# A maximum over eight heads taken in two halves, in the first attention of a four-layer kernel

## The chip, the cores and the metric

The kernel is one program on one core of a Trainium2 chip. Its five engines run their own queues and meet through semaphores: TensorE (PE in the rows, its weight loads PEld) multiplies, VectorE (DVE), ScalarE (ACT) and GpSimd (POOL) work on tiles, and SyncE (SP) issues most transfers. The metric is the device time of one execution in microseconds.

## What is computed

Four layers run one after the other: an attention with relative positions, a deep feed-forward and local-attention stack, a causal attention and a mixture of experts. Only the first is touched:

```python
B, S, D = x.shape                      # 16, 256, 128; H = 16 heads of hd = 8
q, k, v = (proj(Wq), proj(Wk), proj(Wv))
content = jnp.einsum('bhld,bhmd->bhlm', q, k)
rel_k = jnp.einsum('bhld,lmd->bhlm', q, a_k)
rel_q = jnp.einsum('bhmd,lmd->bhlm', k, a_q)
logits = (content + rel_k + rel_q + pos_pos) * scale
attn = jax.nn.softmax(logits, axis=-1)
out = jnp.einsum('bhlm,bhmd->bhld', attn, v) + jnp.einsum('bhlm,lmd->bhld', attn, a_v)
```

The softmax subtracts the maximum of each row of 256 logits before it takes the exponential.

## The kernel before

The first attention works through 16 sequences of 256 tokens. A sequence has four groups g: two blocks of 128 rows (`lt = g // 2`) by two sets of eight heads (`g % 2`). The logits of a group are a tile of 128 rows by 8 heads by 256 columns in SBUF, `logits`. Every engine's order is written out by hand in its function `sequence`, once for the first, the looped and the last sequence; semaphores with counted values tie the engines together.

For one group the work goes like this. TensorE's `scores` writes the products into four banks (L648, L652, L658), `between` them other work for the next sequence (L570 turns x, L577 projects, L598 spreads the keys). VectorE's `add_keyed` adds them into `logits` in two additions (L908), then `maxima` takes the maximum of all eight heads in one reduction (L913) and multiplies it by the negative scale (L916, called the negative here). ScalarE's `exps` takes eight exponentials, one for each head, in two calls of four (L797), each with a column of `nbias`. TensorE's `turn` transposes four heads at a time (L674), ScalarE's `turns` copies them out (L803), and `outputs` multiplies them with the values (L699). VectorE masks these (L948), sums them (L957, L960) and scales them (L963).

Two banks, the `ring`, serve everything else that TensorE writes: x, the projections, the queries with their keys (L609 and L612, copied out by ScalarE at L814), the outputs `y`, and the spread keys `kb` (L598, masked out by VectorE at L940). Each entry waits until the one two places before it is out. So L598 in group 2 waits for VectorE's L948, as does L570, which turns x for the next sequence.

GpSimd works beside them: `far_keys` copies edge values into the logits of the next sequence (L502, L504, after short operations L497 and L500), L519 builds the diagonal keys once the scores of a group are through, and L537 and L540 place the values.

VectorE's order in a looped sequence: maximum of group 1, `outputs(0)`, group 2 with its maximum, `sums(0)`, `outputs(1)`, `blocks`, `sums(1)`, `blocks`, group 3 with its maximum, `outputs(2)`, `sums(2)`, `blocks` and the additions of the next sequence's group 0, its maximum, `outputs(3)`, `sums(3)`.

Of the kernel before, what the change touches and what calls it, by code (L numbers as in the profile page):

```python
# [21 lines left out]
ALU = mybir.AluOpType  # L22
ACT = mybir.ActivationFunctionType
AX = mybir.AxisListType
# [6 lines left out]
SCALE_A = 1.0 / HD ** 0.5  # L31
# [100 lines left out]
def build_program(nc, T, out):  # L132
    ctx = ExitStack()
    with ctx:
        def sb(stack, name, shape, dt=F32):
            return stack.enter_context(nc.sbuf_tensor(name, shape, dt))

        def sem(name):
            return ctx.enter_context(nc.semaphore(name))
# [101 lines left out]
        with ExitStack() as st:  # L241
# [26 lines left out]
            logits = sb(st, "a_logits", [P, LT, H, S])  # L268
# [8 lines left out]
            nmax = sb(st, "a_nmax", [P, 8])  # L277
            nbias = sb(st, "a_nbias", [P, 8])
# [23 lines left out]
            with nc.Block() as block:  # L302
# [130 lines left out]
                def _(pe):  # L433
# [8 lines left out]
                    for i in range(6):  # L442
# [22 lines left out]
            score_full, logit_ok, bias_ok, exp_done = (sem("a_score_full"), sem("a_logit_ok"), sem("a_bias_ok"),  # L465
                                                       sem("a_exp_done"))
# [21 lines left out]
            with nc.Block() as block:  # L488
# [64 lines left out]
                def _(pe):  # L553
                    def sequence(part, b):
# [18 lines left out]
                        def project_groups(names, rep):  # L573
                            for name in names:
                                r, full = room(name)
                                for j in range(2):
                                    last = nc.tensor.matmul(r[:, j * S:(j + 1) * S],  # L577
                                                            rep[:, 2 * name[1] + j, :, :].rearrange("p a c -> p (a c)"),
                                                            xT[:, :], start=(j == 0), stop=(j == 1), skip_group_check=True)
                                last.then_inc(full, 1)  # L580

                        def project_v():
                            r, full = room("v")
                            for t in range(LT):
                                last = nc.tensor.matmul(r[:, t * D:(t + 1) * D], xT[:, t * P:(t + 1) * P], wv[:, :],
                                                        start=(t == 0), stop=(t == 1), skip_group_check=True)
                            last.then_inc(full, 1)

                        def spread_block(name):

                            if name is None:
                                return

                            out_of(ks[name[1] // 4])
                            r, full = room(name)
                            for j in range(2):
                                h = 2 * name[1] + j
                                last = nc.tensor.matmul(r[:, j * S:(j + 1) * S], sum_k[:, h % 4, :], k_parts[:, h // 4, :],  # L598
                                                        start=(j == 0), stop=(j == 1), skip_group_check=True)
                            last.then_inc(full, 1)  # L600
# [15 lines left out]
                        def scores(g, seq):  # L616

                            lt, hg = g // 2, g % 2
                            if g == 0:
                                pe.wait_ge(queries_ok, seq + 1)  # L620
                            if lt == 0:
                                pe.wait_ge(diag_ok, seq * 4 + 2 * hg + 2)

                            def between(i):

                                if g == 1 and i == 0:
                                    turn(0, 1)
                                if part != "loop":
                                    return
                                if g == 1 and i in (1, 2):  # L630
                                    project_groups(ks[i - 1:i], wk_rep)
                                if g == 1 and i == 3:
                                    project_v()
                                if g == 3 and i < 2:
                                    spread_block(kb[2 + i])
                                if g == 0:
                                    spread_block(kb[4 + i])

                            o = [score[:, kq, :].rearrange("p (h m) -> p h m", h=8) for kq in range(4)]

                            def contents(kq):

                                if g > 0 or not isinstance(seq, int) or seq > 0:
                                    at = 3 * (seq * 4 + g - 1) + kq // 2 + 1
                                    pe.wait_ge(logit_ok, at)
                                for i in range(2):
                                    hq = 2 * hg + i
                                    nc.tensor.matmul(o[kq][:, 4 * i:4 * i + 4, :], q_parts[:, hq, lt * P:(lt + 1) * P],  # L648
                                                     k_diag[:, 4 * hq:4 * hq + 4, kq * 64:(kq + 1) * 64],
                                                     start=(i == 0), stop=False, skip_group_check=True)  # L650
                                    if kq == 3 - 3 * lt:
                                        last = nc.tensor.matmul(o[kq][:, 4 * i:4 * i + 4, :], e_parts[:, lt, :],  # L652
                                                                k_diag[:, 4 * hq:4 * hq + 4, kq * 64:(kq + 1) * 64],
                                                                start=False, stop=(i == 1), skip_group_check=True)
                                for n in range(4) if kq != 3 - 3 * lt else ():
                                    blk = kq * 4 + n
                                    v = lt * P - blk * LB + S - LB
                                    last = nc.tensor.matmul(o[kq][:, :, n * LB:(n + 1) * LB], eq_tab[:, v:v + P],  # L658
                                                            k_blk[:, 8 * hg:8 * hg + 8, blk * LB:(blk + 1) * LB],
                                                            start=False, stop=(n == 3), skip_group_check=True)  # L660
                                last.then_inc(score_full, 1)

                            for kq in range(4):
                                contents(kq)
                                between(kq)

                        def turn(g, half):
                            pe.wait_ge(exp_done, b * 8 + 2 * g + half + 1)
                            for mt in range(LT):

                                if half == 1:
                                    pe.wait_ge(turn_out, b * 16 + 4 * g + mt + 1)
                                for h in range(4):
                                    last = nc.tensor.transpose(turned[mt][:, h * P:(h + 1) * P],  # L674
                                                               logits[:, g // 2, 8 * (g % 2) + 4 * half + h,
                                                                      mt * P:(mt + 1) * P], ident[:, :])
                                last.then_inc(turn_full, 1)
# [85 lines left out]
                def _(act):  # L763
                    def sequence(part, b, norm=False):
# [26 lines left out]
                            nc.scalar.copy(v_next, r[:, 0:LT * D].rearrange("p (t c) -> p t c", t=LT)).then_inc(free, 1)  # L791

                        def exps(g, half, seq):
                            act.wait_ge(bias_ok, seq * 4 + g + 1)
                            for h in range(4 * half, 4 * half + 4):
                                row = logits[:, g // 2, 8 * (g % 2) + h, :]
                                last = nc.scalar.activation(row, row, ACT.Exp, bias=nbias[:, h:h + 1], scale=SCALE_A)  # L797
                            last.then_inc(exp_done, 1)
# [91 lines left out]
                def _(dve):  # L890
# [4 lines left out]
                    def sequence(part, b, norm=False):  # L895
# [13 lines left out]
                                "p k (h m) -> p h k m", h=8), at, ALU.add).then_inc(logit_ok, 1)  # L909

                        def maxima(g, seq):
                            dve.wait_ge(logit_ok, 3 * (seq * 4 + g) + 2)
                            nc.vector.tensor_reduce(nmax[:, :], logits[:, g // 2, 8 * (g % 2):8 * (g % 2) + 8, :],  # L913
                                                    AX.X, ALU.max).then_inc(logit_ok, 1)
                            dve.wait_ge(logit_ok, 3 * (seq * 4 + g) + 3)
                            nc.vector.tensor_scalar(nbias[:, :], nmax[:, :], -SCALE_A, None, ALU.mult).then_inc(bias_ok, 1)  # L916

                        def add_and_maxima(g, seq):
                            add_keyed(g, seq, 0)
# [1133 lines left out]
        with ExitStack() as st:  # L2053
# [6 lines left out]
            nmax = sb(st, "c_nmax", [P, 2, 4])  # L2060
# [778 lines left out]
```

## Time and profile before

| | us |
|---|---|
| median of 3 runs | 5165.76 |
| lowest, highest | 5158.77, 5169.23 |
| profiled execution | 5161.43 |
| its span | 5159.6 |
| TensorE, VectorE busy over the span | 4641.8 (90%), 3703.7 (72%) |
| ScalarE, GpSimd busy over the span | 3408.9 (66%), 3562.0 (69%) |
| first attention, its 16 sequences | from about 69 to 1110 |

A row of the timeline gives when an instruction (or a run of like ones, x4) started, how long it took, its engine and line, what it writes and reads, and in square brackets how long the engine was idle before it and which instruction ended that. The busy shares are means over four layers with different limits; the first attention is a fifth of the span.

### The profile page before, as it was taken

To read this page: it belongs to the slowest core of one execution; us is meant where nothing else is said; L and a number is where in the kernel's file an instruction comes from. 1 tells how busy PE (TensorE), PEld (TensorE's weight loads), DVE (VectorE), ACT (ScalarE), POOL (GpSimd) and SP (SyncE) were. 2 spreads that over 40 slices of the span, in tenths; PEclk is the share of its full clock that TensorE was granted. 3 is DMA by queue.
4 is the path that set the end of the run, shared out by engine and by line. 5 is a ranking of instruction groups with operands and counts; after the bars stand their busy time and mean duration, and the time that the engine had idled before them with its cause. 6 is when DMAs were issued, how large, how long until landed. Compare 5 with 4: busy or idle time off the path is not lost. (4 is left out here: it accounts for less than half of the span.)

```text
span 5159.6 us, 202579 instructions
## 1 busy us (share of the span) xinstructions
PE 4641.8 (90%) x82160; PEld 3806.8 (74%) x82160; DVE 3703.7 (72%) x7406; ACT 3408.9 (66%) x6468; POOL 3562.0 (69%) x2507
## 2 busy tenths in 40 slices
PE   6888878879999999999999999999999997788879
PEld 4767666667887788878887888788887886555557
DVE  4666666668887788878887888778877885555543
ACT  3555555547777777777777777777777775566664
POOL 3333333349999999999999999999999995222212
PEclk8999999989999999999999999999999998898889
DMA  3333333323222322232223222232223222000000
GB/s 103 90 90 90 91 91 91 91 74 82 69 69 70 86 69 69 68 88 71 68 70 86 71 69 70 73 83 69 69 71 73 69 70 49 1 0 0 0 1 17
DMA packets 500474, 339.02 MB, mean 66 GB/s; under 512 B 222560, under 2 KB 489085, under 8 KB 499214
## 3 DMA queue, kind: packets, MB, share of 16 engines
q1 hardware_dynamic: 493566, 320.55, 24.5%
q10 hardware_dynamic: 6544, 13.18, 0.8%
q8 instruction: 282, 4.62, 0.4%
q14 instruction: 82, 0.66, 0.0%
HBM read 60.06 MB, written 54.58 MB: 22 GB/s over the span
## 5 line engine op out<-in xcount | busy, mean ns | idle before, releaser
L1401 POOL TENSOR_TENSOR b_rnorm<-b_ss,neghalf 128x16 f32<-128x16 f32 x384 | 1119.1, 2914 | 24.2 <-DVE b_ss L1937 20.2
L1397 POOL TENSOR_TENSOR b_rot<-b_t 128x1024 f32<-128x1024 f32 x384 | 910.0, 2370 | 75.5 <-DVE b_t L1926 74.6
L1924 DVE TENSOR_TENSOR b_t<-psum,b_cosg 128x1024 f32<-128x1024 f32 x384 | 469.6, 1223 | 422.9 <-ACT b_sq L1779 416.9
L1408 POOL TENSOR_TENSOR b_qk<-b_rot,b_rnorm 128x1024 f32<-128x1024 f32 x384 | 731.6, 1905 | 42.8 <-POOL b_rnorm L1401 2.7
L1525 PE MATMUL psum<-b_w_hi,b_xT_parts 128*128 128x512 f32 x1152 | 529.4, 460 | 25.8 <-issue 17.6
L1779 ACT ACTIVATE b_sq<-psum 128x1024 f32<-128x1024 f32 x384 | 392.9, 1023 | 222.4 <-PE psum L1530 222.1
L1931 DVE TENSOR_REDUCE b_ss_floor<-b_sq 128x16 f32<-128x1024 f32 x384 | 464.4, 1209 | 0.0
L1530 PE MATMUL psum<-b_w_hi,b_xT_parts 128*128 128x512 f32 x1152 | 461.0, 400 | 0.0
L1526 PE MATMUL psum<-b_w_lo,b_xT_parts 128*128 128x512 f32 x1152 | 457.8, 397 | 1.2 <-issue 1.2
L1612 PE MATMUL psum<-shared,b_oT 128*128 128x128 f32 x3072 | 425.3, 281 | 0.8 <-ACT b_oT L1797 0.8
L1514 PE MATMUL psum<-ident,b_qk 128*128 128x128 f32 x3072 | 408.0, 276 | 10.1 <-DVE b_o L1963 9.9
L1514 PEld LDWEIGHTS psum<-ident,b_qk 128*128 128x128 f32 x3072 | 362.9, 142 | 71.5 <-DVE b_o L1963 19.3
L797 ACT ACTIVATE a_logits<-a_logits,a_nbias 128x256 f32<-128x256 f32 x512 | 216.8, 500 | 287.4 <-DVE a_nbias L916 286.9
L1612 PEld LDWEIGHTS psum<-shared,b_oT 128*128 128x128 f32 x3072 | 379.9, 191 | 27.0 <-issue 1.1
L1802 ACT ACTIVATE b_pr<-b_pr 128x512 f32<-128x512 f32 x384 | 241.9, 630 | 212.7 <-DVE b_pr L1947 195.0
L1963 DVE TENSOR_TENSOR b_o<-psum,b_rs 128x256 f32<-128x256 f32 x768 | 326.2, 425 | 26.4
L1622 PE MATMUL psum<-b_v_win,b_prT 64*32 64x65 f32 x24576 | 336.0, 225 | 5.9 <-issue 5.9
L1593 PE MATMUL psum<-b_kT,b_qTs 64*32 64x64 f32 x24576 | 333.2, 224 | 0.0
L1639 PE MATMUL psum<-b_xnT,b_w 128*128 128x256 f32 (+1 forms) x1152 | 308.2, 390 | 17.2 <-DVE b_hid L1987 2.9
L1593 PEld LDWEIGHTS psum<-b_kT,b_qTs 64*32 64x32 f32 x24576 | 270.5, 105 | 61.3 <-issue 50.1
L1622 PEld LDWEIGHTS psum<-b_v_win,b_prT 64*32 64x32 f32 x24576 | 271.4, 105 | 53.8 <-issue 7.4
L1797 ACT COPY b_oT<-psum 128x512 f32<-128x512 f32 x384 | 232.5, 606 | 111.3 <-PE psum L1560 111.3
(271 smaller groups left out, 11673.1 us busy)
## 6 DMA issues: line engine op xcount, KB each, us to landing
b_v_win<-b_v SPq DMA_DIRECT2D x2304, 65.0 KB
keyed<-shared SPq DMA_DIRECT2D x64, 768.0 KB, 4.1
b_v_win<-b_v SPq DMA_DIRECT2D x1152, 32.5 KB
a_logits<-keyed SPq DMA_DIRECT2D x128, 160.0 KB, 3.2
oa<-XR SPq DMA_DIRECT2D x1024, 2.0 KB
xcur<-X SPq DMA_DIRECT2D x111, 128.0 KB, 4.3
shared<-in_L_ffn_Wqkv_dram ACTq DMA_DIRECT2D x6, 1536.0 KB
a_logits<-keyed SPq DMA_DIRECT2D x64, 128.0 KB, 3.3
```

What stands on the lines that cost most here:

```text
L1397: nc.gpsimd.tensor_tensor(rot[:, i, :, :], t1[:, i, :, :], t2[:, i, :, :], ALU.add).then_inc(rot_done, 1)
L1401: nc.gpsimd.tensor_tensor(rnorm[:, i, :], ss[:, i, :], neghalf[:, :], ALU.pow).then_inc(rn_done, 1)
L1408: nc.gpsimd.tensor_tensor(qk[:, i, :, :], rot[:, i, :, :], rnorm[:, i, :, None].broadcast_to((P, 16, BD)), ALU.mult).then_inc(qk_done, 1)
L1514: last = nc.tensor.transpose(r[:, p * P:(p + 1) * P], qk[:, s % 2, a * 8 + 2 * p:a * 8 + 2 * p + 2, :].rearrange("p h d -> p (h d)"), iden ...
L1525: nc.tensor.matmul(r, xT_hi[:, ts], w_hi[:, piece(hg, i)], start=True, stop=False)
L1526: nc.tensor.matmul(r, xT_hi[:, ts], w_lo[:, piece(hg, i)], start=False, stop=False)
L1530: return nc.tensor.matmul(r, xT_lo[:, ts], w_hi[:, piece(hg, i)], start=False, stop=True)
L1593: last = nc.tensor.matmul(bank[3 + j][qs, p * 2 * WIN:(p + 1) * 2 * WIN], qTs[at, p, qs], kT[at, p, keys], start=False, stop=(p == 3), ski ...
L1612: last = nc.tensor.matmul(bank_c[:, 0:D], oT[:, p, :], wo[:, 4 * (s % SEQ // 2) + p, :], start=(p == 0), stop=(p == 3))
L1622: last = nc.tensor.matmul(r[qs, p * (BD + 1):(p + 1) * (BD + 1)], prT[at, p, qs], v_win[at, s % NV, c, p, :], start=(p == 0), stop=(p == 3 ...
L1924: nc.vector.tensor_tensor(t14, x4, tab(cosg, slice(0, BD), BD), ALU.mult)
L1931: nc.vector.tensor_reduce(ss_floor[:, t, :, 0], sq[:, :].rearrange("p (h d) -> p h d", d=BD), AX.X, ALU.add).then_inc(ss_done, 1)
```

## The change

The maximum is taken over four heads, then its negative, then the same for the other four. `bias_ok` counts two per group instead of one, so that the exponentials of a half wait for their own negative, and `logit_ok` counts four instead of three, which renumbers TensorE's wait in `contents`. The bytes read and written are the same; VectorE has two more instructions per group, 128 in all.

```diff
@@ TensorE, contents
-                                    at = 3 * (seq * 4 + g - 1) + kq // 2 + 1
+                                    at = 4 * (seq * 4 + g - 1) + kq // 2 + 1
@@ ScalarE, exps
-                            act.wait_ge(bias_ok, seq * 4 + g + 1)
+                            act.wait_ge(bias_ok, 2 * (seq * 4 + g) + half + 1)
@@ VectorE, maxima
-                            dve.wait_ge(logit_ok, 3 * (seq * 4 + g) + 2)
-                            nc.vector.tensor_reduce(nmax[:, :], logits[:, g // 2, 8 * (g % 2):8 * (g % 2) + 8, :],
-                                                    AX.X, ALU.max).then_inc(logit_ok, 1)
-                            dve.wait_ge(logit_ok, 3 * (seq * 4 + g) + 3)
-                            nc.vector.tensor_scalar(nbias[:, :], nmax[:, :], -SCALE_A, None, ALU.mult).then_inc(bias_ok, 1)
+                            for half in range(2):
+                                hs = slice(4 * half, 4 * half + 4)
+                                dve.wait_ge(logit_ok, 4 * (seq * 4 + g) + 2 + half)
+                                nc.vector.tensor_reduce(nmax[:, hs], logits[:, g // 2, 8 * (g % 2) + 4 * half:
+                                                                            8 * (g % 2) + 4 * half + 4, :],
+                                                        AX.X, ALU.max).then_inc(logit_ok, 1)
+                                dve.wait_ge(logit_ok, 4 * (seq * 4 + g) + 3 + half)
+                                nc.vector.tensor_scalar(nbias[:, hs], nmax[:, hs], -SCALE_A, None,
+                                                        ALU.mult).then_inc(bias_ok, 1)
```

VectorE's queue in the looped sequences, from the last addition of group 0 to the masking of the outputs of group 3, before (in the changed kernel the lines behind stand four higher, so L948 is L952 there):

```order
184 L908 TENSOR_TENSOR a_logits<-psum,a_logits 128x8x128
185 L912 ISA
186 L913 TENSOR_REDUCE a_nmax<-a_logits 128x8
187 L915 REGISTER_ALU
188 L916 TENSOR_SCALAR a_nbias<-a_nmax 128x8
189 L898 REGISTER_ALU
190 L948 TENSOR_TENSOR a_ymask<-psum,a_own 128x432 x2
```

The same place in the changed kernel:

```order
211 L908 TENSOR_TENSOR a_logits<-psum,a_logits 128x8x128
212 L914 ISA
213 L915 TENSOR_REDUCE a_nmax<-a_logits 128x4
214 L918 REGISTER_ALU
215 L919 TENSOR_SCALAR a_nbias<-a_nmax 128x4
216 L915 TENSOR_REDUCE a_nmax<-a_logits 128x4
217 L918 REGISTER_ALU
218 L919 TENSOR_SCALAR a_nbias<-a_nmax 128x4
219 L898 REGISTER_ALU
220 L952 TENSOR_TENSOR a_ymask<-psum,a_own 128x432 x2
```

A second maximum and a second negative stand between the first negative and the masking; nothing else changes its place on any engine.

## Rows read from the trace of the kernel before

**Rows 1.** The head of the page: the span of the whole execution.

```profile
span 5159.6 us, 202579 instructions
```

**Rows 2.** Windows, 69 to 1110: busy us of each engine, PEclk, DMA, GB/s.

```profile
69.00:1110.00 1041.00, 836.12 (x12340) 725.08 (x12344) 692.41 (x907) 532.40 (x1171) 329.46 (x506) 0.93 0.32 89
```

**Rows 3.** By line: duration min/median/max in ns, or busy us and mean ns.

```profile
L913 DVE TENSOR_REDUCE a_nmax<-a_logits x64: 2286/2286/2286, 77.7 to 1099.9; 128x8 f32<-128x2048 f32 x64
...
L916 DVE TENSOR_SCALAR a_nbias<-a_nmax x64: 171/188/617, 80.0 to 1102.2; 128x8 f32<-128x8 f32 x64
...
L1931 DVE TENSOR_REDUCE b_ss_floor<-b_sq 128x16 f32<-128x1024 f32 x384 | 464.4, 1209 | 0.0
```

**Rows 4.** Timeline, group 2 of one sequence, all engines: start us, us, engine, line.

```profile
305.64 3.75 POOL L519 TENSOR_TENSOR a_k_diag<-a_k_parts,a_head_rows 128x1024 fp32r<-128x1024 f32 x2 [2.13 <-PE psum L658]
306.85 2.29 DVE L913 TENSOR_REDUCE a_nmax<-a_logits 128x8 f32<-128x2048 f32 x1
309.17 0.24 DVE L916 TENSOR_SCALAR a_nbias<-a_nmax 128x8 f32<-128x8 f32 x1
309.36 1.69 DVE L957 TENSOR_REDUCE a_ysum<-a_ymask 128x72 f32<-128x864 f32 x1
309.45 3.31 ACT L797 ACTIVATE a_logits<-a_logits,a_nbias 128x256 f32<-128x256 f32 x8 [7.12 <-DVE a_nbias L916]
...
311.20 1.09 PE L674 MATMUL psum<-ident,a_logits 128*128 128x128 f32 x8 [3.03 <-ACT a_logits L797]
...
312.81 0.30 PEld L598 LDWEIGHTS psum<-a_k_parts,a_sum_k 128*128 128x128 f32 x2 [0.28 <-DVE a_ymask L948]
...
313.27 0.90 PEld L674 LDWEIGHTS psum<-ident,a_logits 128*128 128x128 f32 x8 [0.17 <-ACT a_probsT L803]
```

**Rows 5.** Timeline, group 0, a sequence where the negative met GpSimd's copies early.

```profile
536.91 2.34 POOL L537 COPY a_values<-shared 128x544 f32<-128x544 f32 x4
536.97 0.60 DVE L916 TENSOR_SCALAR a_nbias<-a_nmax 128x8 f32<-128x8 f32 x1
537.48 1.11 DVE L948 TENSOR_TENSOR a_ymask<-psum,a_own 128x432 f32<-128x432 f32 x2
```

**Rows 6.** Timeline, group 3 of the sequence of rows 4.

```profile
318.83 3.75 POOL L519 TENSOR_TENSOR a_k_diag<-a_k_parts,a_head_rows 128x1024 fp32r<-128x1024 f32 x2 [9.44 <-PE psum L658]
...
320.05 2.29 DVE L913 TENSOR_REDUCE a_nmax<-a_logits 128x8 f32<-128x2048 f32 x1
...
322.81 1.25 POOL L502 COPY a_logits<-shared 128x1280 f32<-128x1280 f32 x1
...
323.20 0.61 DVE L948 TENSOR_TENSOR a_ymask<-psum,a_own 128x432 f32<-128x432 f32 x1 [0.60 <-PE psum L699]
...
323.87 0.45 PE L609 MATMUL psum<-a_ek_diag,a_q_next 128*128 128x384 f32 x1 [0.18 <-DVE a_ymask L948]
```

**Rows 7.** Timeline, group 0 of the next sequence; last, TensorE's loop turning over.

```profile
271.82 2.29 DVE L913 TENSOR_REDUCE a_nmax<-a_logits 128x8 f32<-128x2048 f32 x1
...
273.04 2.34 POOL L537 COPY a_values<-shared 128x544 f32<-128x544 f32 x4
...
274.14 0.17 DVE L916 TENSOR_SCALAR a_nbias<-a_nmax 128x8 f32<-128x8 f32 x1
274.24 1.12 DVE L948 TENSOR_TENSOR a_ymask<-psum,a_own 128x432 f32<-128x432 f32 x2
...
274.90 0.44 PE L570 MATMUL psum<-ident,xcur 128*128 128x128 f32 x2 [2.10 <-DVE a_ymask L948]
...
276.10 1.97 PE L674 MATMUL psum<-ident,a_logits 128*128 128x128 f32 x8 [0.77 <-ACT a_logits L797]
...
406.86 0.68 PE L570 MATMUL psum<-ident,xcur 128*128 128x128 f32 x2 [4.34 <-issue]
```

**Rows 8.** Timeline, TensorE: transposes in a looped sequence (group 2) and the last one.

```profile
443.61 1.97 PE L674 MATMUL psum<-ident,a_logits 128*128 128x128 f32 x8 [3.03 <-ACT a_logits L797]
...
1090.11 1.09 PE L674 MATMUL psum<-ident,a_logits 128*128 128x128 f32 x8 [2.97 <-ACT a_logits L797]
```

## The prediction

> **What bounds the kernel now.** The profiled execution spans 5159.6 us [rows 1] and took 5161.4; the median of the runs shown is 5165.8. The change touches the first attention alone, 69 to 1110 us of the trace, so I read that stage. By the windows TensorE is busy 836 of 1041 us there, VectorE 692, ScalarE 532, at a mean granted clock of 0.93 [rows 2]: no engine is full, and the stage goes at the pace of a chain that passes from one engine to the next. The next view is therefore the timeline of one sequence (about 64.8 us; there are 16, four groups each), read for what each TensorE wait is put down to. Three places matter:
>
> - Group 2: the maximum ends, the negative follows, ScalarE starts its eight exponentials at 309.45, TensorE transposes from 311.20. Behind that stands the row to notice: the loads of L598 wait for VectorE's L948, up to 312.81, and only 0.17 us of waiting for ScalarE is left at 313.27 [rows 4]. VectorE's own queue (maximum, L957, L948) is already the last to arrive at L598, and at the next transposes ScalarE and VectorE come in almost together.
> - Group 3: L609 waits for L948 at 323.87, and ScalarE's copies of what L609 makes stand ahead of the second half's exponentials in its queue [rows 6].
> - Group 0 of the next sequence: VectorE's L948 frees the bank in which TensorE turns x (L570, a wait of 2.10 us), then the transposes wait 0.77 us for ScalarE [rows 7].
>
> **The change, part by part.** *Pieces.* One maximum of 2286 ns becomes two of 1024 elements. L1931, another reduction, of 1024 elements, takes 1209 ns [rows 3]; 2286 is 2048 elements and a rest, so two halves are 2.42 to 2.44 us: 0.15 dearer. The negative's shortest is 171 ns [rows 3], and one follower starts about 0.10 us behind it at 274.24 [rows 7] (the negative stands at 274.14, 2.32 us after the maximum began). So undisturbed, the first negative ends 1.25 + 0.17 = 1.42 us after the maximum starts, where now it is 2.49: **1.07 us earlier**. The work behind it starts at 2.71 instead of 2.42: **0.29 us later**. The second half's negative (2.8) is there before the first four exponentials are through (1.42 + 1.62, four of eight in 3.3 us). The two waits for numbers of the semaphore are renumbered and hold nobody back.
>
> *Who stands beside it.* In groups 2 and 3 GpSimd runs L519, two operations in 3.75 us, started by the same end of the scores that starts VectorE's last addition: 305.64 for a maximum at 306.85. The negative at 309.17 takes 0.24, not 0.17, and ends at 309.41, when L519 ends (309.39) [rows 4]. At 536.97 it takes 0.60 us and ends with the first of four copies of L537 (one is 0.6 us), begun 0.06 us ahead of it; L948 behind it starts only then [rows 5]. I read this as: the negative waits until GpSimd's operation is over, and VectorE's queue waits with it. Before, all but 0.07 us of that was covered by the length of the maximum itself. The split moves the first negative 1.07 us forward, into the middle of the operation. The longest hold that a row shows is 0.60 - 0.17 = 0.43; a negative that starts at 308.10 and ends with L519 at 309.41 would be held for 1.31 - 0.17 = 1.14. Bounds for one such hold: 0 and 1.14; I take all of it, since every row ends with the GpSimd operation however it began.
>
> The Trainium skill has this as a rule ("SBUF — State Buffer", section "SBUF: two separate sides"): VectorE and GpSimd share a pair of ports as an exclusive lock, and the loser blocks for the whole instruction; it names VectorE operations in a two-port mode and those with two inputs in SBUF. "VectorE: DVE Perf Modes", section "Mode 2×_2P — use both read ports for one tensor", puts an fp32 tensor_scalar from SBUF to SBUF in that mode. The trace agrees by the 0.24 and 0.60 above. By the rule the sum is the one below; without it, that of the first rival.
>
> *Group 2.* The first half ends at 308.07, its negative is held to 309.41, where the whole one ends today: the exponentials gain nothing. The second half runs 309.36 to 310.6, its negative after L519 is free, and L957 starts at 310.70 instead of 309.36: VectorE is 1.34 us late. L948, and with it the loads of L598, come at 314.15 instead of 312.81; their own 0.29 brings the transposes of the second half to 314.44 instead of 313.27: **+1.2 us**. That is the case in 11 of 15 sequences. In the other four TensorE does the eight transposes at half speed, 1.97 us [rows 8] instead of 1.09, and comes some 0.5 us later to L598, so VectorE's lateness costs about **0.75**. Sum 13.2 + 3.0 = 16.2 us.
>
> *Group 3.* L519 and the maximum move by the same 1.2 us and lie alike: the first negative is again held to L519's end (323.8), the second half ends at 325.0, and its negative meets L502, a copy of 1.25 us that begins then 0.2 us behind L519 (322.81 today, 324.01 then) and is held to 325.28. L948 starts near 325.25 instead of 323.20: 2.05 late, 0.85 more than TensorE. L609 has to wait for it. Of this some 0.2 is taken back, as the first four exponentials no longer delay ScalarE's copies. I take **+0.6**, between 0 and 1.0: 9.0 us in 15 sequences.
>
> *Group 0.* The half ends 1.22 us after the start, exactly where L537 begins (273.04 for 271.82). As at 536.97 the first negative is held to the first copy's end: ready at 1.87 instead of 2.49. The second lands between copies and ends at about 3.2, L948 starts 0.7 us later (0.3 to 1.1), L570 at 275.6 instead of 274.90. TensorE no longer waits the 0.77 us for ScalarE, so the transposes start at 275.9 instead of 276.10: **-0.2** (-0.6 to +0.35), 12 times: -2.4. At two further turns TensorE's own loop holds L570 for 4.34 us [rows 7], and nothing changes.
>
> *Group 1* of the 15: the first exponentials start earlier, but TensorE's L609 and ScalarE's copies set the pace behind; 0.
>
> *First and last sequence.* Here nothing of VectorE is behind the transposes: TensorE waits 2.97 us for the exponentials at 1090.11 [rows 8], more in the first sequence, and GpSimd is idle: 1.07 gained four times, 0.6 once (group 0 with L537 beside it): -4.9.
>
> **Sum** 16.2 + 9.0 - 2.4 - 4.9 = **+17.9 us**: 5179.3 against 5161.4, and 5183.7 on the median. ScalarE's and GpSimd's instructions stay; SP's stores and reads stay in order and move with the sums. The later stages keep their instructions.
>
> **Rivals.**
>
> (1) *Faster: the negative isn't held.* If a 128x4 negative slips in beside L519, VectorE is only 0.29 us late. Group 2 then still doesn't gain (L598 waits on VectorE: about +0.1), group 3 gains 0.2, group 0 gains 0.6 x 12 = 7, the ends 5.3: 13 us, and about 2 more where the shorter wait spares TensorE its half speed: 5150. For it: at 274.14 a negative ran in 0.17 while L537's copies ran. Against: it stood at the seam of two copies (1.10 us after the first began, and four take 2.34), and each negative beside L519 in groups 2 and 3 ends with it. It decides when the hold is under some 0.3 us. Chance 0.13.
>
> (2) *No difference: the clock gives it back.* TensorE's granted clock falls to half after its waits, in two places in nearly every sequence: the eight transposes at 276.10 take 1.97 us, those at 1090.11 take 1.09. The mean of 0.93 over 1041 us [rows 2] is 0.07 x 2 x 1041 = 146 us at the lower level, 1.2 GHz, and 73 us of work not done in them. Waits that move by 2 us per sequence can lose some of these stretches or gain some. A seventh of them lost is 10 us and brings +18 to +8, inside what can be told apart; as much gained brings +28. A smaller hold in group 3 (0 instead of 0.6) also ends at +9. Chance 0.23, time near 5172.
>
> (3) *The hold is dearer*: both group 0 (+0.35) and group 3 (+1.0) at their upper ends and 1.34 in each group 2: 20 + 15 + 4 - 5 = +34, 5200. It is part of the forecast's side.
>
> **How the numbers follow.** The forecast with (3) has 0.64. A measurement of this kernel tells about 0.2% (10 us) from no change. Slower by over 0.2%: 0.64, within: 0.23, faster: 0.13. The predicted time is 5184. The range reaches from 5157 (below rival 2, most of rival 1 left out) to 5202 (rival 3).
>
> **What would show it.** In the timeline of the changed kernel, first negatives of groups 2 and 3 of 1.1 to 1.3 us that end with L519, and second negatives of group 3 held by L502; if the longest is under 0.3 us, rival 1 holds. The exponentials of group 2 start no earlier against the maximum's start (2.6 us after it), and TensorE's wait in front of L598 grows from 0.28 us to over 1 us. In group 0 L570's wait grows from 2.10 to near 2.8, and the 0.77 for ScalarE goes. The last sequence is 4 us shorter. A sequence of the loop takes 66.3 us instead of 64.8. The prediction is wrong in its main step if sequences are as long as now or shorter, and wrong by the clock if holds are as said, yet the stage's mean clock is far from 0.93.

## The result, and the profile after

The changed kernel takes 5200.43 us (median of 4 executions, 5197.28 to 5209.0), the kernel before 5162.92 (4, with one more run than above): a ratio of 1.0074, with an interval of 1.0057 to 1.0092. It is slower by 37.5 us. The forecast was slower, at 5184, in a range up to 5202. The profiled execution took 5200.61, against 5161.43. One number further down needs a word: of the twelve executions of the kernel in which ScalarE makes the negatives, one took 7589 us at a mean granted clock of 0.77 (the others had 0.95 to 0.96), and it is left out of that kernel's ratio.

First the page of the changed kernel: its span [rows 1], and the busy time of the engines with the count of their instructions.

```profile
span 5198.8 us, 202811 instructions
...
PE 4655.9 (90%) x82160; PEld 3825.4 (74%) x82160; DVE 3749.8 (72%) x7534; ACT 3409.6 (66%) x6468; POOL 3562.2 (69%) x2507
```

VectorE has 128 instructions more and is busy 46 us longer; TensorE has the same number of matmuls and is busy 14 us longer, as part of them run at a lower clock. The last run of products (L699) of the first attention starts at 1146.59 us of the trace, where it started at 1112.83: 33.8 of the 39.2 us of longer span arise in this stage. The same view as [rows 2], over the changed kernel's stage (PEclk is the third figure from the end, 0.90):

```profile
69.00:1147.00 1078.00, 859.37 (x12433) 752.05 (x12432) 737.47 (x1036) 532.22 (x1169) 327.36 (x502) 0.90 0.31 85
```

The mean granted clock fell from 0.93 to 0.90. By line, as [rows 3], duration min/median/max in ns:

```profile
L915 DVE TENSOR_REDUCE a_nmax<-a_logits x128: 1205/1218/1222, 73.1 to 1137.2; 128x4 f32<-128x1024 f32 x128
...
L919 DVE TENSOR_SCALAR a_nbias<-a_nmax x128: 170/333/1375, 74.4 to 1138.5; 128x4 f32<-128x4 f32 x128
```

Two halves are 2.44 us, as worked out. The negative of four elements, whose shortest is 170 ns, takes up to 1375. The timeline of one ordinary sequence shows where it is long. First group 2, as [rows 4] (start us, us, engine, line; idle time and its end in brackets).

```profile
580.46 3.75 POOL L519 TENSOR_TENSOR a_k_diag<-a_k_parts,a_head_rows 128x1024 fp32r<-128x1024 f32 x2 [2.14 <-PE psum L658]
581.67 1.22 DVE L915 TENSOR_REDUCE a_nmax<-a_logits 128x4 f32<-128x1024 f32 x1
...
582.93 1.31 DVE L919 TENSOR_SCALAR a_nbias<-a_nmax 128x4 f32<-128x4 f32 x1
584.15 1.21 DVE L915 TENSOR_REDUCE a_nmax<-a_logits 128x4 f32<-128x1024 f32 x1
584.27 3.30 ACT L797 ACTIVATE a_logits<-a_logits,a_nbias 128x256 f32<-128x256 f32 x8 [7.12 <-DVE a_nbias L919]
585.39 0.17 DVE L919 TENSOR_SCALAR a_nbias<-a_nmax 128x4 f32<-128x4 f32 x1
585.57 1.71 DVE L961 TENSOR_REDUCE a_ysum<-a_ymask 128x72 f32<-128x864 f32 x1
...
586.03 1.97 PE L674 MATMUL psum<-ident,a_logits 128*128 128x128 f32 x8 [3.03 <-ACT a_logits L797]
...
588.48 1.08 PEld L598 LDWEIGHTS psum<-a_k_parts,a_sum_k 128*128 128x128 f32 x4 [0.88 <-DVE a_ymask L952]
588.48 1.37 PE L598 MATMUL psum<-a_k_parts,a_sum_k 128*128 128x256 f32 x4 [0.48 <-DVE a_ymask L952]
```

L519 ends at 584.21, and so does the negative (584.24). The exponentials start 2.60 us after the maximum did, as before, and L961 3.90 us after it, where L957 started 2.51 after: VectorE is 1.39 us late. The transposes start 4.36 us after the maximum, as before (4.35), but take 1.97 us instead of 1.09. Group 3, as [rows 6]:

```profile
596.29 3.75 POOL L519 TENSOR_TENSOR a_k_diag<-a_k_parts,a_head_rows 128x1024 fp32r<-128x1024 f32 x2 [12.08 <-PE psum L658]
...
598.76 1.30 DVE L919 TENSOR_SCALAR a_nbias<-a_nmax 128x4 f32<-128x4 f32 x1
...
600.28 1.26 POOL L502 COPY a_logits<-shared 128x1280 f32<-128x1280 f32 x1
...
601.22 0.33 DVE L919 TENSOR_SCALAR a_nbias<-a_nmax 128x4 f32<-128x4 f32 x1
...
602.12 0.45 PE L609 MATMUL psum<-a_ek_diag,a_q_next 128*128 128x384 f32 x1 [0.96 <-DVE a_ymask L952]
```

The first negative ends with L519 (600.04), the second with L502 (601.54), and L609 waits 0.96 for L952 where it waited 0.18. Group 0 of the next sequence, as [rows 7]:

```profile
615.90 2.34 POOL L537 COPY a_values<-shared 128x544 f32<-128x544 f32 x4
615.92 0.63 DVE L919 TENSOR_SCALAR a_nbias<-a_nmax 128x4 f32<-128x4 f32 x1
616.47 1.21 DVE L915 TENSOR_REDUCE a_nmax<-a_logits 128x4 f32<-128x1024 f32 x1
...
617.71 0.55 DVE L919 TENSOR_SCALAR a_nbias<-a_nmax 128x4 f32<-128x4 f32 x1
618.17 1.11 DVE L952 TENSOR_TENSOR a_ymask<-psum,a_own 128x432 f32<-128x432 f32 x2
...
618.82 0.44 PE L570 MATMUL psum<-ident,xcur 128*128 128x128 f32 x2 [3.16 <-DVE a_ymask L952]
```

Both negatives are held, each to the end of a copy of L537 (616.5, and 618.24 with the last), and L570 waits 3.16 instead of 2.10. The wait of 0.77 in front of the transposes is gone.

**A sequence against a sequence**, both from one L570 to the next (274.90 to 339.76 before, 550.49 to 618.82 after): 64.86 us became 68.33.

The starts that bound the stretches are 274.90, 300.55, 311.20, 320.26, 334.97 and 339.76 before, and 550.49, 575.38, 586.03, 597.73, 612.97 and 618.82 after.

| stretch | before | after | differs | forecast |
|---|---|---|---|---|
| L570 to the transposes of group 1's second half | 25.65 | 24.89 | -0.76 | -0.2 less what is late at L570 |
| to group 2's transposes | 10.65 | 10.65 | 0 | 0 |
| to the L609 of group 3 that waits 0.81 for ScalarE | 9.06 | 11.70 | +2.64 | +1.2 |
| to the first L699 of group 3 | 14.71 | 15.24 | +0.53 | +0.6 |
| to the next L570 | 4.79 | 5.85 | +1.06 | +0.7 |

One stretch is far from its forecast, the one that holds group 2's transposes. The granted clock there, in windows of 1 us of TensorE (us, busy, PEclk), of the changed kernel and then of the kernel before, each around its transposes (586.03 and 311.20):

```profile
584.00:585.00 1.00, 0.00 (x0) 1.00 0.00 0
585.00:586.00 1.00, 0.00 (x0) 0.66 0.00 0
586.00:587.00 1.00, 0.97 (x5) 0.50 0.00 0
...
591.00:592.00 1.00, 1.00 (x7) 0.50 0.07 4
592.00:593.00 1.00, 1.00 (x10) 0.92 0.07 4
```

```profile
310.00:311.00 1.00, 0.00 (x0) 1.00 0.00 0
311.00:312.00 1.00, 0.80 (x7) 1.00 0.00 0
312.00:313.00 1.00, 0.90 (x6) 1.00 0.03 2
```

Behind the same wait of 3.03 us (3.1 in the first two sequences) the changed kernel's TensorE runs some 6.8 us at the lower level, 1.2 GHz, in 14 of 15 sequences, and 3.4 in the other; before, it stayed at 2.4 GHz in 11 of 15, and the other four had 3.4 us. In two of the changed kernel's sequences, at 242.45 and 309.97, the clock falls 1.5 and 2.3 us after the transposes started, and these take 1.09 us; there L598 waits 1.37 us for VectorE, a second wait that the kernel before doesn't have in any sequence. From 60 us to the end of the stage, summed from windows of 0.5 us, TensorE spent 214.7 us at the lower level in 46 stretches, against 158.0 in 39.

### The profile page after: what moved, and what is told of

The parts are those of the page before. It is cut to its first block and busy times, and to the rows that moved or that the text cites. A ratio compares the mean times of both kernels' runs of the same rounds, so it can differ in the third digit from the quotient of the medians.

```text
span 5198.8 us, 202811 instructions
## 1 busy us (share of the span) xinstructions
PE 4655.9 (90%) x82160; PEld 3825.4 (74%) x82160; DVE 3749.8 (72%) x7534; ACT 3409.6 (66%) x6468; POOL 3562.2 (69%) x2507
```

## The experiments

Each is compared with executions of the kernel before that were timed beside it: their median was 5164.65 for the three kernels with one group halved and the one with ScalarE's negatives, 5164.04 for the next four, and 5165.14 for the four with added products. Theories: **A**, the hold of the negative by GpSimd's running operation makes VectorE late, and TensorE waits for that; **B**, the two halves or their waits cost by themselves, wherever they stand. The clock became a third question after the first traces; the expectations call it theory C: about half of the loss is TensorE at the lower clock behind group 2's wait.

### One group alone

The maxima of one group halved, of the others whole (the numbers on the semaphores follow), in 15 of the 16 sequences. The edit against the kernel before, with `(2,)`, `(3,)` or `(0,)`, shortened:

```diff
+            HALVED, HALVED_FIRST, HALVED_LAST = (2,), False, False
...
-                            nc.vector.tensor_reduce(nmax[:, :], logits[:, g // 2, 8 * (g % 2):8 * (g % 2) + 8, :],
+                            parts = (slice(0, 4), slice(4, 8)) if halved(g, seq) else (slice(0, 8),)
+                            for n, hs in enumerate(parts):
...
```

> Only group 2 of the looped sequences is halved (15 times). Theory A (the first negative is held by GpSimd's L519, so VectorE comes 1.34 us late to L598, and TensorE, waiting longer, loses more at half speed): about 2.6 us a sequence as in the changed kernel's trace, +39 us; the hold without the clock would be 1.2 a sequence, +18. Theory B (two more VectorE instructions per group cost what they cost, 0.29 us, GpSimd has no part): under +5 us.

> Only group 3 is halved (15 times). Theory A: both negatives are held, L609 waits for VectorE, +0.5 to +0.6 us a sequence, +9 us. Theory B: the first exponentials come 0.8 us earlier and the copies behind with them, -3 us to 0.

> Only group 0 of the looped sequences is halved (15 times). Theory A: held by L537's copies, L570 one us late, some of it given back as TensorE no longer waits for the exponentials: +0.3 us a sequence, 0 to +10 us. Theory B: -0.6 us a sequence, -8 us.

Measured: group 2 alone 5199.19 us, ratio 1.0067 [1.0045, 1.0088], **+34.5**; group 3 alone 5186.71, 1.0051 [1.0035, 1.0066], **+22**; group 0 alone 5166.22, 1.0006 [0.9998, 1.0015], **+1.6**. Group 2 is near what A expected with the clock in it (+39). Group 3 costs more than twice its forecast, and the three come to 58 where all together cost 37.5: the medians don't add. In the stage of group 3's kernel the windows give 200 us at the lower clock in 45 stretches, where the kernel before has 158 in 39, and not at group 3 alone: from 614.8 the clock is low for 6.8 us behind group 0's wait, which the edit doesn't touch, where the kernel before has 3.4. Halves that meet a copy of 0.6 us (group 0) cost next to nothing. B had expected under +5, at most 0, and -8 us: it is wrong in groups 2 and 3, and group 0's interval leaves its -8 out as well.

### VectorE late, without halves

Maxima whole, and behind the negative of group 2 a reduction that nobody reads:

```diff
+                            if g in (2,):
+                                nc.vector.tensor_reduce(idle[:, :], own[:, None, :].broadcast_to((P, 10, YW)),
+                                                        AX.X, ALU.max)
```

> The kernel before with whole maxima, and behind the negative of each group 2 a VectorE reduction of 1080 elements of a constant into a tile that nobody reads (about 1.28 us): VectorE is as late there as in the change, with no halves and no held negative. Theory A (only VectorE's lateness counts): the same as the kernel that halves group 2 alone, +35 to +40 us for 16 groups. If the held negative or the halves do more than make VectorE late: under +20 us.

Measured: 5193.03 us, 1.0058 [1.0044, 1.0072], **+29**. VectorE and TensorE in group 2:

```profile
584.66 1.26 DVE L919 TENSOR_REDUCE a_idle<-a_own 128x10 f32<-128x1080 f32 x1
585.85 1.70 DVE L961 TENSOR_REDUCE a_ysum<-a_ymask 128x72 f32<-128x864 f32 x1
```

```profile
586.54 1.68 PE L675 MATMUL psum<-ident,a_logits 128*128 128x128 f32 x8 [3.03 <-ACT a_logits L798]
588.74 1.37 PE L599 MATMUL psum<-a_k_parts,a_sum_k 128*128 128x256 f32 x4 [0.52 <-DVE a_ymask L952]
```

An ordinary 1.19 us of lateness (584.66 to 585.85) costs 29 us where group 2's halves alone cost 34.5. That is under the +35 to +40 expected, and so is the lateness under the 1.39 us of the changed kernel; it is well over the +20 below which the halves or the hold would have had a cost of their own. So most of the loss is lateness, whatever makes it, and it is paid for dearly: 1.8 us per sequence for 1.19. Here too TensorE runs at the lower clock behind group 2's wait in all 15 looped sequences: in nine the transposes are slowed (1.64 to 1.97 us), in six they take 1.09 and the clock falls 1.0 to 2.4 us after they started, in the wait of L599 for VectorE or just behind it.

### The holder shortened

GpSimd's L519 over 32 of its 256 columns in the loop, with whole maxima and with halved ones. These two leave out the rest of the diagonal keys.

```diff
-                            nc.gpsimd.tensor_tensor(k_diag[:, hq * 4:hq * 4 + 4, :],
...
+                            w = S if part == "first" else 32
+                            nc.gpsimd.tensor_tensor(k_diag[:, hq * 4:hq * 4 + 4, 0:w],
...
```

> The kernel before with GpSimd's L519 over 32 of 256 columns in the looped sequences (the keys of the other columns are left as the first sequence wrote them, which leaves work out): it is over long before any negative. L519 is on nobody's path: -3 to +1 us against the kernel before.

> The changed kernel with the same shortened L519 (work left out as in the kernel with whole maxima). Theory A: groups 2 and 3 have no held first negative, the loss of some 45 us there goes, what is left is group 0 (+5) and the gain of the ends (-5): within 5 us of the kernel before, at best -10. Theory B: still +25 us or more.

Measured: whole 5199.19 us, 1.0066 [1.0052, 1.0079], **+35**; halved 5152.94, 0.998 [0.9971, 0.9989], **-11**. The second is as A had it: the first negatives of groups 2 and 3 are free, and the change loses nothing, though group 3's second negatives are still held by L502 (0.8 us in most sequences). GpSimd also has less work there, so this run alone doesn't prove A. The first is a plain miss. Its trace shows a hold that wasn't foreseen. GpSimd and VectorE in group 3 (L917 is the negative, L914 the maximum there):

```profile
599.19 1.25 POOL L502 COPY a_logits<-shared 128x1280 f32<-128x1280 f32 x1
```

```profile
597.09 2.29 DVE L914 TENSOR_REDUCE a_nmax<-a_logits 128x8 f32<-128x2048 f32 x1
599.41 1.06 DVE L917 TENSOR_SCALAR a_nbias<-a_nmax 128x8 f32<-128x8 f32 x1
```

L502 stands behind L519 in GpSimd's queue. With L519 short it starts before the maximum is through instead of behind the negative, and holds the negative for 1.06 us, to its own end (600.44 against 600.47). Here is the kernel before, without any halving, with a negative of 1.0 to 1.2 us in group 3 of all 15 looped sequences, and its ordinary sequences last 68.2 us instead of 64.8. In the one from 550.95 on, 2.4 of these 3.4 us lie in group 3 (17.1 us from the L609 that waits for ScalarE to L699, before 14.7), with a stretch at the lower clock in them that the kernel before doesn't have there. The hold was moved by the experiment, not taken away. That all 35 us come from it is argued, not shown.

### Only where GpSimd is idle

Halved: the first group of the first sequence, and groups 1 to 3 of the last.

```diff
+            HALVED, HALVED_FIRST, HALVED_LAST = (), True, True
```

> Only the first group of the first sequence and groups 1 to 3 of the last are halved, where GpSimd is idle and TensorE waits 3 us or more for the exponentials. Both theories: four times -1.07 us, -4 us, at the edge of what can be measured; read from the trace: 1.07 us earlier from the maximum's start to the exponentials.

Measured: 5162.31 us, 0.9993 [0.9984, 1.0002], **-1.7**, inside what can't be told from nothing; the forecast of -4 isn't refuted. Its trace has what was to be read from it: the exponentials start 1.46 us after the maximum in these four groups, where they started 2.53 after it before, 1.07 earlier. In the changed kernel the last sequence, from the transposes of group 0 on, runs 46.9 us instead of 51.6 (1099.65 to 1146.59 and 1061.26 to 1112.83): its halves gain there, as forecast, but TensorE also spends 6.6 us less at the lower clock in it, so not all of the 4.6 us need be theirs.

### ScalarE makes the negatives

All maxima halved, and the negative taken from VectorE's queue:

```diff
+                                act.wait_ge(logit_ok, before_group(g, seq, 3) + 3 + n)
+                                nc.scalar.mul(nbias[:, hs], nmax[:, hs], -SCALE_A).then_inc(bias_ok, 1)
...
-                            nc.vector.tensor_scalar(nbias[:, :], nmax[:, :], -SCALE_A, None, ALU.mult).then_inc(bias_ok, 1)
```

> All groups are halved as in the change, but ScalarE makes the negatives (a multiplication ahead of its four exponentials). Nothing of VectorE can be held by GpSimd there any more, and VectorE's queue is 0.1 us longer than before instead of 1.3. Theory A: the loss is gone and the earlier exponentials show, -5 to -15 us against the kernel before. Theory B, or a cause in the halves or in the earlier exponentials: slower than before, +15 us or more.

Measured: 5155.75 us, 0.9979 [0.9969, 0.999], **-9**, against +37.5 for the same halves with VectorE's negatives. In group 2, across ScalarE and TensorE:

```profile
569.38 0.20 ACT L820 ACTIVATE a_nbias<-a_nmax 128x4 f32<-128x4 f32 x1 [5.78 <-DVE a_nmax L942]
569.62 1.71 ACT L824 ACTIVATE a_logits<-a_logits,a_nbias 128x256 f32<-128x256 f32 x4
```

```profile
571.38 1.09 PE L696 MATMUL psum<-ident,a_logits 128*128 128x128 f32 x8 [1.93 <-ACT a_logits L824]
573.42 1.37 PE L617 MATMUL psum<-a_k_parts,a_sum_k 128*128 128x256 f32 x4 [0.94 <-DVE a_ymask L976]
```

Beside the same running L519 ScalarE's negative takes 0.20 us, and the transposes wait 1.93 instead of 3.03. So the split does what it says as soon as its negatives are not VectorE's: 45 us against the change. (The profiled execution took 5164.39 us, 9 over the median.)

### TensorE kept at work in its waits

To separate the clock from the hold, products that nobody reads were put into TensorE's waits: 16 in front of group 2's transposes in the changed kernel and in the kernel before; in the kernel before also 12 in front of L570, where TensorE waits 2.10 us, and 10 in front of the L609 behind group 1's scores, where it waits 1.87; and 12, 10 and 10 in the kernel in which ScalarE makes the negatives. They write to a bank of the transposes, so the 10 have a wait for ScalarE's copies of group 0 ahead of them.

```diff
+                        def idle_products(count):
+
+                            for _ in range(count):
+                                nc.tensor.matmul(turned[0][:, 0:2 * KJ].rearrange("p (h j) -> p h j", h=2), unit[:, :],
+                                                 pp_parts[:, None, :].broadcast_to((P, 2, KJ)),
+                                                 start=True, stop=True, skip_group_check=True)
...
+                        idle_products(16)
```

> The changed kernel with 16 products that nobody reads (2.8 us at full speed) in TensorE's wait of 3.03 us ahead of group 2's transposes. What they fill is idle time, so the hold of VectorE stays as it is. Theory C (half of the loss is TensorE at half speed behind that wait, 6.8 us of it in each sequence): the stretches at group 2 go, and the kernel is 15 to 20 us faster than the changed one, about +16 us on the kernel before. If the whole loss is VectorE's lateness: no change, +37 us.

> The kernel before with the same 16 products at the same place. Only 4 of its sequences have the half-speed stretch there, 0.6 us each: -2 us under theory C, 0 otherwise; more than +5 would say that the products themselves cost something and weaken the other run.

> The kernel before with products that nobody reads in all three waits of TensorE: 12 ahead of turning x (2.1 us), 10 ahead of L609 (1.9 us), 16 ahead of group 2's transposes. Theory C: the 3.4 us at half speed behind each of the first two waits go in each sequence, 0.8 us saved in the transposes and about as much in the products of L577, up to 1 us at L609: -20 to -35 us. If half speed there is off the path: 0, and up to +5 where a product overruns a wait.

> Halves with ScalarE's negatives and products that nobody reads in the three waits (12, 10 and 10, as the wait at group 2 is 1.9 us here). Theory C: the gains add, -9 and -20 to -35: 5120 to 5135 us. If the waits or the half speed are not what bounds this one: near 5155.

| kernel | median us | ratio [interval] | against before |
|---|---|---|---|
| change, 16 products | 5165.60 | 1.0009 [0.9997, 1.0021] | +0.5 |
| before, 16 products | 5153.84 | 0.9983 [0.9970, 0.9995] | -11 |
| before, products in three places | 5148.53 | 0.9975 [0.9963, 0.9987] | -17 |
| ScalarE's negatives, products in three places | 5108.70 | 0.9895 [0.9880, 0.9910] | **-56** |

The changed kernel with 16 products, group 2, TensorE:

```profile
575.76 3.07 PE L725 MATMUL psum<-a_pp_parts,a_unit 128*128 128x384 f32 x16
578.87 1.09 PE L674 MATMUL psum<-ident,a_logits 128*128 128x128 f32 x8
581.33 0.30 PEld L598 LDWEIGHTS psum<-a_k_parts,a_sum_k 128*128 128x128 f32 x2 [1.60 <-DVE a_ymask L960]
581.33 1.08 PE L598 MATMUL psum<-a_k_parts,a_sum_k 128*128 128x256 f32 x4 [1.37 <-DVE a_ymask L960]
...
589.18 0.44 PE L609 MATMUL psum<-a_ek_diag,a_q_next 128*128 128x384 f32 x1 [0.82 <-ACT shared L822]
```

```profile
578.00:579.00 1.00, 0.96 (x6) 1.00 0.00 0
579.00:580.00 1.00, 0.96 (x8) 1.00 0.00 0
580.00:581.00 1.00, 0.00 (x0) 1.00 0.00 0
```

For VectorE nothing differs: the negative is held as before (1.30 us), the transposes start 4.36 us after the maximum, and the wait for VectorE at L598, 1.37 us, is now in the open. But the transposes take 1.09 us in all 15 looped sequences, and in 13 of them the clock stays at 2.4 GHz up to group 3. The change had lost 37.5 us; with the wait filled it is level with before. The products help the kernel before too (-11); its time at the lower clock falls from 158 to 128 us.

This splits group 2's term. From its transposes to the L609 that waits for ScalarE (578.87 to 589.18 here) there are, over 14 looped sequences of each kernel:

| kernel | us | seen in |
|---|---|---|
| before | 9.06 | 10 of 14; 9.6 to 9.9 in the four with slow transposes |
| before, 16 products | 9.05 to 9.13 | all |
| change | 11.5 to 12.8, mean 11.8 | all |
| change, 16 products | 10.1 to 10.3 | 12 of 14; 11.9 in the two where the clock falls later |

With the clock held up, VectorE's lateness costs 1.0 to 1.3 us a sequence; the rest of the loss there, about 1.4 us, is TensorE at the lower clock. Over the whole time, the two kernels with the wait filled lie 11.8 us apart by the medians, 18.4 by the spans of their profiled executions (5168.3 and 5149.9): the cost of the holds without the lower clock behind group 2's wait. By this difference the other 19 to 26 of the 37.5 us are that clock.

My expectation for the changed kernel (+16) was too high, that for the kernel before too small with products in one place (-2 expected), and too hopeful with products in three (-20 to -35). For the last the trace shows a cause. The products move the turns of the engines a little, and now group 1's negative meets a copy of GpSimd's (of three rows, GpSimd's, VectorE's and TensorE's):

```profile
551.77 1.25 POOL L504 COPY a_logits<-shared 128x1280 f32<-128x1280 f32 x1
551.87 1.18 DVE L929 TENSOR_SCALAR a_nbias<-a_nmax 128x8 f32<-128x8 f32 x1
553.61 0.44 PE L609 MATMUL psum<-a_ek_diag,a_q_next 128*128 128x384 f32 x1 [1.16 <-DVE a_ymask L961]
```

Group 1's negative takes 1.17 to 1.26 us in 15 of 16 sequences, where it took 0.17 before, and this L609 waits 1.16 us instead of 0.19. So -17 is a gain by the clock less a new hold. The last kernel has its negatives on ScalarE and so no such hold; it is the fastest of the study, and beats its forecast. Its windows over 14 sequences:

```profile
78.00:952.00 874.00, 778.77 (x11400) 678.80 (x11399) 600.29 (x809) 494.13 (x1159) 295.90 (x453) 1.00 0.34 93
```

TensorE is at 2.4 GHz nearly throughout, and sequences last 60.2 to 64.0 us, with a first period of 66.4. That is more than the two parts bring alone (-9 and -17), which the new hold in the one and the lower clock in the other explain at least in part: from 60 us on its stage has 37 us at the lower level, that of the kernel with ScalarE's negatives has 199 (in its profiled execution), that of the kernel before with products in three places 73.

## Why the prediction came out as it did

The direction and its cause were right, the size short by half: +17.9 forecast, +37.5 measured, inside the range by 2 us. That it is inside is luck: the upper end was rival 3's sum of dearer holds, and the loss came to that size by the clock. What the sum did price, holds with the clock unchanged, measured 12 to 18 us between the two kernels with group 2's wait filled.

- **The hold** is shown as the prediction put it. First negatives of groups 2 and 3 take 1.30 to 1.38 us and end with L519, second ones of group 3 are held by L502, and beside an idle GpSimd the same instruction takes 0.17. I took all of the 1.14 between 0 and 1.14: right. The loss fell away on ScalarE (-9 instead of +37.5) and with a short L519 (-11).
- **Pieces**: two halves take the 2.44 us worked out, and the exponentials of group 2 start no earlier.
- **Group 2** is the step that failed. The term was +1.2 in 11 sequences and +0.75 in four, which took the four that show half speed as given and the other eleven as staying at full speed. It measured +2.64 in the sequence shown. VectorE's 1.39 us of lateness is there, and with the clock held up it costs the +1.0 to +1.3 that was forecast; the transposes at 1.97 instead of 1.09 and everything behind them up to 592.2 at 1.2 GHz are what was missing. The wait of L598's loads grew from 0.28 to 0.88 us only (the products' to 0.48), not to over 1, because the slow transposes covered the rest; with the clock held up it is 1.60 (1.37). That sign of the prediction, taken alone, would have spoken against the right theory.
- **Group 3**: +0.53 against +0.6. In the sum of one sequence the term holds; as an experiment of its own it costs 22 us instead of 9, with 42 us more at the lower clock, part of it behind waits of other groups.
- **Group 0**: the path to L570 is 1.06 late (0.7 forecast, bounds 0.3 to 1.1), since the second negative is held as well; -0.76 comes back behind it. The net is +0.30 where -0.2 stood, inside its bounds; alone it measured +1.6 us.
- **Ends**: the last sequence is 4.6 us shorter from its group 0 on, some of it perhaps by the clock; the 1.07 us is in the trace, and timed alone the ends give -1.7, not to be told from zero.
- **Rival 1** (not held) is refuted by the rows. **Rival 2** named the right quantity and put the wrong sign first: the lower clock took 56.7 us more of the stage instead of giving some back. A seventh of 146 more, its losing side, had been priced at +28; it was over a third. **Rival 3** named +34 and came nearest to the size, but by another way: only group 0's hold is near its upper end, and what it put on the other holds is the clock's.

The mistake has a plain form: the sum priced a wait and its lateness at the mean clock, and then let the clock vary as a rival of its own. It should have stood in the term of group 2, since the trace already held its two cases: transposes of 1.09 and of 1.97 us after the same 3.03 us of waiting [rows 8], 11 and 4 times. The four could become fifteen, and did, once two of them are counted in which the clock falls only behind the transposes.

What stays open is why a TensorE that waits the same 3.03 us drops its clock in one kernel and keeps it in the other. The rows show that it does, that work in the wait prevents it, and that the kernels with a late VectorE have a second wait, at L598, right behind it: where the transposes there still took 1.09 us, the clock fell beside that second wait. What decides between the two, no run here shows. The Trainium skill ("TensorE: Matmul & The Clock Gate", section "HAM oscillation — how this bites in real kernels") describes a kernel in which the work behind each wait for a transfer starts at the lower clock, every time. The changed kernel is close to that (the transposes slowed behind the wait in 13 of 15 sequences, the clock low within 2.3 us of their start in the other two); the kernel before, with the same wait and 1.09 in 11 of 15, is not.

## What to carry to other kernels

A tiny VectorE scale behind a long instruction can cost as much as is left of the GpSimd operation that runs when it starts: before cutting the long one, lay GpSimd's queue beside the new start, or give the tiny one to ScalarE. The same look is due when anything else moves: two of the experiments here brought such a meeting about in another group. Where TensorE waits 2 to 3 us in every turn of a loop, a lateness of 1.2 to 1.4 us cost 1.0 to 1.3 with the clock held up, and 1.8 to 2.6 without; look at windows of 1 us behind each wait, count both cases, and price the worse one. A few products that nobody reads, in such waits, tell the clock's part from the rest, and here they paid for themselves.

## What the runs showed of the hardware that was not expected

- A VectorE fp32 scale of 4 or 8 elements, 0.17 us alone, is held by any GpSimd operation in these traces, one with two inputs (L519: 1.30 to 1.38 us) and plain copies (L537: 0.55 and 0.63; L502: 0.33, 1.06; L504: up to 1.26). In the twelve traces in which VectorE makes the negatives there are 1009 of them, and none that began beside a running GpSimd operation ended before it (to within 0.03 us). The reductions beside it are not held: L915 is 1205 to 1222 ns in 128 executions. ScalarE's scale of the same elements stays at 0.19 to 0.21, and 48 of the 128 in the kernel with ScalarE's negatives end before the GpSimd operation that was running.
- Costs of separate places didn't add: +34.5, +22 and +1.6 alone, +37.5 together. Ordinary sequences moved in steps, as stretches of some 3.4 us at the lower clock came or went: 64.8 us with two of them, 68.3 with four (at 551.2, 564.9 and a double one at 585.3).
- 3.07 us of products that nobody reads, in a wait that is there anyway, brought 35 us in the changed kernel and 11 in the kernel before; with the negatives on ScalarE the products in three places brought 47 (5155.75 to 5108.70). In the kernel before, the same three places brought only 17, as the products moved a negative onto GpSimd's copy.
